# Attention inside a fused transformer layer: sums behind the second half's scores, maxima between the halves, the last two PSUM banks paired anew

## The reference

```python
xn = _layernorm(x)
q, k, v = split(einsum('bte,fe->btf', xn, in_proj))        # 16 heads of 8
a = softmax(q / sqrt(8) @ k.T + causal mask)
attn = (a @ v) @ out_proj.T
w = top-2 of softmax(xn @ wr.T + rb), normalised
ffn = expert_shared(xn) + sum_e w[:, e] * expert_e(xn)     # silu(h@g.T) * (h@u.T) @ d
out = x + attn + ffn
```

## Time and profile before

| | |
|---|---|
| time, median of 3 runs | 467.42 us (467.25 to 471.32) |
| profiled execution, span from first to last instruction | 485.8 us |
| front, to the first exponential | 44.3 us |
| attention, 64 steps | about 226 us |
| experts, from the last exponential | about 216 us |
| PE busy / DVE / ACT / POOL | 439.9 / 359.8 / 312.8 / 302.7 us |

### The profile page before, as it was taken

The page is one execution under the profiler, slowest core; times in us unless marked ns, Lnnn a source line. Parts: engine busy times, 40 slices in busy tenths (PEclk is TensorE's granted clock), DMA queues, the critical chain, the costliest instruction groups (busy, mean ns, idle before and its releaser), DMA issues.

```text
span 485.8 us, 12527 instructions
## 1 busy us (share of the span) xinstructions
PE 439.9 (91%) x3983; PEld 329.3 (68%) x3987; DVE 359.8 (74%) x804; ACT 312.8 (64%) x709; POOL 302.7 (62%) x439
## 2 busy tenths in 40 slices
PE   8888897988998989999889999998999899979995
PEld 4666565665666666666555688786877788868884
DVE  6885997987878877778774387585765777566987
ACT  2756676775867677767677676565565766555552
POOL 1326887997887888887888500755547487845300
PEclk9999999998999999999999999999999999989998
DMA  8776798999875555666356337787777767821762
GB/s 233 229 240 233 230 329 294 295 332 331 266 232 153 156 164 174 173 177 168 119 165 255 90 84 214 242 290 225 225 234 247 239 195 258 299 60 35 245 204 65
DMA packets 60415, 102.00 MB, mean 210 GB/s; under 512 B 11045, under 2 KB 29226, under 8 KB 59328
## 3 DMA queue, kind: packets, MB, share of 16 engines
q1 hardware_dynamic: 55872, 92.74, 61.2%
q0 software_dynamic: 4480, 8.47, 5.2%
HBM read 62.49 MB, written 39.46 MB: 210 GB/s over the span
## 4 chain that ended last, share of the span: by engine, by line
PE 62%; ACT 7%; POOL 6%; issue 5%; DVE 4%; SPq 4%; DMA 2%; another core or an unknown queue 2%; DVEq 0%; ACTq 0%; POOLq 0%
PE ps L850 11%; PE ps L848 11%; PE ps L849 11%; PE ps L917 6%; PE ps L978 6%; PE ps L925 4%; ACT sb_work L706 4%; POOL sb_work L620 3%; POOL xs L596 2%; PE ps L998 2%; DMA sb_ring<-qk 2%; PE ps L1143 2%; PE ps L981 2%; SPq L471 2%
## 5 line engine op out<-in xcount | busy, mean ns | idle before, releaser
L1343 DVE TENSOR_REDUCE sb_blockmax<-ps 128x6 f32<-128x768 f32 x128 | 121.5, 956 | 37.2 <-PE ps L925 32.4
L706 ACT ACTIVATE sb_work<-ps 128x768 f32<-128x768 f32 x128 | 104.7, 818 | 64.7 <-PE ps L913 63.5
L648 POOL DMA_INDIRECT ys<-sb_v_all,sb_xn_all x76 | 81.3, 1069 | 72.3 <-DVE sb_v_all L1464 52.6
L620 POOL TENSOR_SCALAR_AFFINE_SELECT sb_work<-sb_work 128x512 f32<-128x512 f32 x128 | 82.2, 646 | 27.6 <-ACT sb_work L706 25.5
L849 PE MATMUL ps<-sb_ring,sb_wb 128*128 128x512 f32 (+1 forms) x231 | 83.6, 362 | 0.0
L1443 DVE TENSOR_TENSOR sb_v_all<-ps,sb_v_all 128x512 f32<-128x512 f32 (+1 forms) x93 | 57.5, 618 | 24.4 <-ACT sb_v_all L796 10.6
L596 POOL DMA_INDIRECT xs<-sb_xn_all,sb_posu x64 | 62.9, 983 | 10.6 <-issue 10.6
L917 PE MATMUL ps<-sb_ring 32*128 32x256 f32 x256 | 49.5, 377 | 20.7 <-ACT sb_work L706 10.1
L796 ACT ACTIVATE sb_v_all<-ps 128x512 f32<-128x512 f32 (+1 forms) x93 | 49.7, 534 | 10.5 <-PE ps L850 5.4
L917 PEld LDWEIGHTS ps<-sb_ring 32*128 32x128 f32 x256 | 25.6, 183 | 44.9 <-issue 38.4
L848 PE MATMUL ps<-sb_ring,sb_wb 128*128 128x512 f32 (+1 forms) x138 | 51.6, 374 | 3.3 <-issue 1.8
(11 more groups left out here) (168 smaller groups left out, 1089.0 us busy)
## 6 DMA issues: line engine op xcount, KB each, us to landing
sb_wb<-wd SPq DMA_DIRECT2D x75, 384.0 KB
sb_ring<-qk SPq DMA_DIRECT2D x64, 256.0 KB
wd<-sb_wb SPq DMA_DIRECT2D x8, 1152.0 KB, 5.9
xs<-sb_o_all SPq DMA_DIRECT2D x19, 260.0 KB, 4.2
qk<-sb_ring SPq DMA_DIRECT2D x32, 128.0 KB
sb_work<-ys SPq DMA_DIRECT2D x16, 256.0 KB, 3.2
sb_xn_all<-xs SPq DMA_DIRECT2D x15, 260.0 KB
sb_o_all<-w SPq DMA_DIRECT2D x8, 384.0 KB, 3.9
```

Source lines behind the costliest of these rows:

```text
L620: pool.affine_select(out=o, in_=o, compare_op=ALU.is_ge, fill=0.0, base=0, pattern=[[0, 4], [1, 128]], channel_multiplier=-1)\
L648: pool.indirect_dma_start(out=ys_d, out_offset=bass.IndirectOffsetOnAxis(ap=row, axis=0), in_=yst[i % NYS][:, EMB * j:EMB * j + EMB], in_o ...
L706: act.activation(part.rearrange("p (k h q) -> p h k q", h=2, q=128), ps[:, 4:6, 0:HEAD].rearrange("p h (k q) -> p h k q", q=128), ACT.Exp, ...
L1343: dve.tensor_reduce(blockmax[:, a:b + 1, 0:3], ps[:, a:b + 1, 0:HEAD].rearrange("p h (k c) -> p h k c", c=128), AX.X, ALU.max).then_inc(s[ ...
```

## The change

The banks are paired anew: X becomes bank 6 and J bank 7. Sums go to X beside the transposes, and side products go to J beside the maxima (the last sums, of n = 63, go to J). On PE `sums(n - 1)` moves from before `scores(n, 1)` to behind it. `maxima` moves from the end of step n, where it served quad n + 2, to between the halves, where it serves quad n + 1. On ACT the copy of the queries moves between the two exponentials, the copy of the sums no longer waits for the maxima but comes behind the side copy, and the copy of the values moves from n mod 4 = 0 to n mod 4 = 2 of the sequence before. No instruction is added or removed; DVE, POOL and SP keep their order.

```diff
-        J, X = ps[:, 6, :], ps[:, 7, :]
+        X, J = ps[:, 6, :], ps[:, 7, :]
...
+        def summed_out(n):
+            return (X if n < NQ - 1 else J)[:, 256:512]
...
+            def summed(n):
+                act.wait_ge(s["PV"], n + 1)
+                if isq(n - 1):
+                    act.wait_ge(s["T"], n)
+                act.activation(ot[:, :], summed_out(n), ACT.Copy).then_inc(s["OT"], 1)
...
                     for k, pair in enumerate(PAIRS[::-1]):
-                        if k and isq(n - 2):
-                            unscaled(n - 2)
+                        if k:
+                            if isq(n - 2):
+                                unscaled(n - 2)
+                            queries(n + 1)
                         act.wait_ge(s["ST"], 2 * n + k + 1)
...
+                if isq(n - 1):
+                    summed(n - 1)
                 c = turned(n)
...
-                if isq(n - 1):
-                    act.wait_ge(s["PV"], n)
-                    if isq(n + 2):
-                        act.wait_ge(s["Mt"], n + 3)
-                    if isq(n - 2):
-                        act.wait_ge(s["T"], n - 1)
-                    act.activation(ot[:, :], J[:, 256:512], ACT.Copy).then_inc(s["OT"], 1)
-                if n >= 0:
-                    queries(n + 2)
...
             def step(n):
...
-                if n == 0:
-                    maxima(1)
                 if isq(n - 2):
-                    bank_read(n - 1)
                     pe.wait_ge(s["OT"], n - 1)
...
                     last.then_inc(s["T"], 1)
+                if isq(n) and isq(n + 1):
+                    maxima(n + 1)
+                if isq(n) or isq(n + 3):
+                    scores(n, 1)
                 if isq(n - 1):
                     sums(n - 1)
-                if isq(n) or isq(n + 3):
-                    scores(n, 1)
                 if n > -4:
                     bank_read(n - 1)
-                if isq(n - 2) and has_side(n):
-                    pe.wait_ge(s["xc"], n - 1)
-                side(n)
-                if n >= 0 and isq(n + 2):
-                    maxima(n + 2)
+                if has_side(n):
+                    if isq(n):
+                        pe.wait_ge(s["q4b"], min(n + 2, NQ))
...
+                    side(n)
```

More of the change, by code:

```diff
@@ L692, in unscaled, with own_values @@
                 act.activation(xo[c % 2][:, :, j, :, :], view[:, :, :, 0:HD + 1], ACT.Copy).then_inc(s["xc"], 1)
+            def summed(n):
[3 more added lines that the diff above has]
+                act.activation(ot[:, :], summed_out(n), ACT.Copy).then_inc(s["OT"], 1)
+            def own_values(b):
+                act.wait_ge(s["lg"], b + 1)
+                act.wait_ge(s["v1"], 2)
+                if b >= 2:
+                    act.wait_ge(s["PV"], 4 * (b - 1))
+                act.activation(v_sb[b % 2][:, :, :, 0:HD],
+                               v_all[:, 2 * b:2 * b + 2, :].rearrange("p s (h d) -> p s h d", h=HEADS), ACT.Copy)\
+                    .then_inc(s["va"], 1)
             def step(n):
@@ L708, in step @@
                                        scale=SCALE).then_inc(s["ex"], 1)
-                        if n == 0 and k == 0:
-                            queries(1)
                 if j in (0, 1) and isb(b + 3):
@@ L729, in step @@
                         .then_inc(s["cnt"], 1)
-                if isq(n - 1):
-                    act.wait_ge(s["PV"], n)
-                    if isq(n + 2):
-                        act.wait_ge(s["Mt"], n + 3)
-                    if isq(n - 2):
-                        act.wait_ge(s["T"], n - 1)
-                    act.activation(ot[:, :], J[:, 256:512], ACT.Copy).then_inc(s["OT"], 1)
-                if n >= 0:
-                    queries(n + 2)
-                if j == 0 and isb(b):
-                    act.wait_ge(s["lg"], b + 1)
-                    act.wait_ge(s["v1"], 2)
-                    if b >= 2:
-                        act.wait_ge(s["PV"], 4 * (b - 1))
-                    act.activation(v_sb[b % 2][:, :, :, 0:HD],
-                                   v_all[:, 2 * b:2 * b + 2, :].rearrange("p s (h d) -> p s h d", h=HEADS), ACT.Copy)\
-                        .then_inc(s["va"], 1)
+                if n == 0:
+                    own_values(0)
+                if n >= 0 and j == 2 and isb(b + 1):
+                    own_values(b + 1)
                 if n == 2:
@@ L970, in sums @@
                 b, j = quad(n)
-                if isq(n + 2):
-                    pe.wait_ge(s["q4b"], n + 3)
+                if isq(n - 1):
+                    pe.wait_ge(s["xc"], n)
+                    pe.wait_ge(s["OT"], n)
                 pe.wait_ge(s["sel"], 2 * n + 2)
@@ L976, in sums @@
                 p = P[n % 2].rearrange("p (a k h q) -> p a h k q", a=2, h=2, q=128)
+                out = summed_out(n)
                 for h in range(4):
-                    pe.matmul(J[32 * h:32 * h + 32, 256:512], v_sb[b % 2][:, 0, 4 * j + h, :],
+                    pe.matmul(out[32 * h:32 * h + 32, :], v_sb[b % 2][:, 0, 4 * j + h, :],
                               p[:, h // 2, h % 2, 1:3, :], start=True, stop=False, skip_group_check=True)
                 for h in range(4):
-                    last = pe.matmul(J[32 * h:32 * h + 32, 384:512], v_sb[b % 2][:, 1, 4 * j + h, :],
+                    last = pe.matmul(out[32 * h:32 * h + 32, 128:256], v_sb[b % 2][:, 1, 4 * j + h, :],
                                      p[:, h // 2, h % 2, 0, :], start=False, stop=True,
@@ L1023, in tokens_across, with idle @@
                 last.then_inc(s["xT"], 1)
-            def idle(count):
+            def idle(count, out=J):
                 for _ in range(count):
-                    pe.matmul(X[:, :], busy[:, 0:128], busy[:, :], start=True, stop=True, skip_group_check=True)
+                    pe.matmul(out[:, :], busy[:, 0:128], busy[:, :], start=True, stop=True, skip_group_check=True)
             pe.wait_ge(s["busy"], 1)
@@ L1054, in _ @@
             maxima(0)
-            idle(2)
+            idle(2, X)
             pe.wait_ge(s["lg"], NB)
```

9 lines of the change are left out of this document (5 added, 4 removed).

## The result

The changed kernel takes **472.23 us** in the median of 20 runs (470.4 to 474.9), the kernel before on the same chip 467.15 us (20 runs, 465.11 to 471.32). The ratio is 1.0104, with a 95% interval of 1.0083 to 1.0125: **slower by 1%**, 5.1 us, where 3.0 us less was forecast. The time lies above the range, 457 to 471.

A forecast was written before the change was run, and what follows sets the result against it. Attention steps were taken as bound by mask, sums and scores in series, and by ACT where a side product stands. Gains 2.1 + 0.8 + 0.9 + 0 - 0.2 - 0.6 = 3.0 us: 467.4 to 464.4 us, range 457 to 471.

The forecast's parts named there:

- part three: Steps with n mod 4 = 2 and 3 take 3.15 and 3.25 us; a four-step sequence 13.70 against 13.83 now.
- the zero for steps 0 to 23: No gain, as DVE's routing and transfers hold these steps; bounds a gain of 4 us and a loss of 2.
- So 6 x 0.13 = 0.8 us gained: Steps 28 to 51: six sequences fall from 13.83 to 13.70 us each.
- 0.9 in steps 24 to 27: This one sequence falls from 14.60 to 13.70 us, 0.9 gained.
- steps 52 to 60: Nine steps without side product, POOL their floor, at 3.20 us: 28.8 against 30.9, 2.1 us gained.
- Rival B: VectorE's late remainder delays maxima and second scores in 26 side steps, 0.4 us each: 10.4 us more, 474.8; chance 0.13.
- the side steps: Steps with a side product (n mod 4 = 0 or 1, to n = 49): second half 2.15 us, held by ACT.
- In steps 61 to 63 ... I take 0.2.: Sums stand in front of the first expert's matmuls: a 0.2 us loss, at most 0.79.
- Step 34's 0.6: Second exponential 2.61 us after the first, ACT idle for PE, cause unknown: about 0.6 us expected to be paid again.
- the first half: From a step's first exponential to its second: 1.50 us, no longer waiting for POOL's mask and the sums.
- Rival A: ACT does not hold side steps, whose second half ends with PE at 1.87 us: 7.3 us more gained, 457.1; chance 0.22.
- Rival C: The loop gets no shorter, the halves exchanging what they have: 467.4 us, give or take 1; chance 0.13.

The follow-up runs named there:

- experiment 5: Changed kernel with VectorE's routing piece moved from between the two maxima to the step's end: 494.13 us, 1.0218; with side product ahead of sums too, 488.19 us, 1.011.
- after: First profile of the changed kernel, no further edit: span 472.7 us; median of its timed runs 472.23 us.
- before_again: Kernel before, unchanged, profiled again on a chip of the 485 us sort: 485.2 us against 486.03, ratio 1.000.
- experiment 4: Changed kernel with VectorE's small reductions of the maxima ahead of the side product's remainder: 494.17 us, 1.012, and 493.0 us, 1.0143.
- before_two: Kernel before, unchanged, profiled on a chip of the 467 us sort: 467.52 us, ratio 1.0035, span 465.2 us.
- before: Profile of the kernel before that the forecast was made from, on a chip of the 485 us sort: span 485.8 us.
- side_first_three: Changed kernel with the side product ahead of the sums on PE, on a chip of the 485 us sort: 490.73 us, 1.0101.
- neg_first_two: Changed kernel with VectorE's small reductions of the maxima ahead of the side product's remainder, second run: 493.0 us against 483.61, 1.0143.
- route_last: Changed kernel with VectorE's routing piece moved to the step's end: 494.13 us against 482.63, 1.0218.
- best_again: Changed kernel with side product ahead of sums, ACT's turned copy ahead of the sums' copy, values' copy between the exponentials: 482.69 us, 0.9993.
- best_third: Changed kernel with side product ahead of sums, ACT's turned copy ahead of the sums' copy, values' copy between the exponentials: 487.87 us, 1.0048.
- ot_first: Changed kernel with ACT's sums' copy ahead of its side copy: 493.19 us against 486.03, 1.0114.

## Why the prediction was wrong

**The steps that failed are the subtraction in part three and the zero for steps 0 to 23.**

*"So 6 x 0.13 = 0.8 us gained", and 0.9 in steps 24 to 27.* The minuend came from one execution, 18.4 us above the median that was to be predicted, and I took it that its surplus lay elsewhere. Part of it lay here. On the chip of 467 us a sequence before takes 81.11 / 6 = 13.52, not 13.83, and steps 24 to 27 take 13.91, not 14.58. Against 13.83 measured for the changed kernel that is 6 x 0.31 = 1.9 us lost, and 0.1 gained. The minuend was mis-sized by 1.9 and 0.7, the changed kernel's own term by 0.8 (13.70 for 13.83). In steps 52 to 60 both were mis-sized alike, 30.9 for 30.20 and 28.8 for 27.70, and the difference came out nearly right by that. Even the trace that I had showed how thin this term was: 0.13 in 13.8.

*"I take 0" for steps 0 to 23, "nearest to the loaded engines", with a loss of 2 at the most.* Measured are 3.8. The bound of 2 priced twelve side products at 0.15 each and nothing else. The side steps' second halves lose more than that even in the quiet stretch: 2.20 for 1.91 with n mod 4 = 0 and 2.19 for 1.60 with n mod 4 = 1, which the forecast never compared. The other second halves lose 0.27 and 0.37. So the second halves of steps 0 to 23 lose 6.9 us. In steps 28 to 51 the first halves give 7.2 back; here they give 3.1. "DVE's routing and the transfers hold them, and the order on both is unchanged" was true and beside the point: what VectorE does is unchanged, but the changed kernel asks for its result earlier. Before, the maxima for the queries after next stood last in a step; now those of the next queries stand ahead of the second scores, so a delay of VectorE's small reductions lands on the exponentials. The first halves of steps 12, 15, 16 and 20 take 2.22 + 2.31 + 2.64 + 2.13 = 9.30 us, against 7.84 before and 5.8 without routing pieces in front (experiment 5). So 1.5 us of the loss is the change's, nearly all of it in steps 15 and 16 (1.71 and 1.67 before); in steps 12 and 20 the kernel before had long first halves too, 2.04 and 2.42.

The granted clock blurs the split of the 3.8. The changed kernel had 0.53 in step 16's second half (3.33 us, where `after` took 2.20); the kernel before had 0.77 in steps 0 and 1 (7.41 us, where `before_again` took 6.19 at 1.00). Three executions of before took 41.64 to 44.27 us in steps 0 to 11, two of the changed kernel 43.71 and 47.28. So each row of the table is known to about 1 us there.

Rival B named this mechanism, VectorE coming late for the maxima and the second scores, but I priced it only where the remainder delays it, in the side steps of a quiet stretch. There it does not occur, as forecast. In steps 12 and 15 it does (experiment 4).

*"In steps 61 to 63 ... I take 0.2."* Behind the last exponential 1.1 us are lost. The new wait in front of the sums makes step 63's sums wait for ACT's unscaled copy (L696), and ACT does the table load and an instruction of the experts first. The changed kernel:

```profile
266.85 0.81 ACT L729 ACTIVATE sb_work<-ps 128x768 f32<-128x768 f32 x1 [0.51 <-PE ps L923]
268.40 1.28 ACT L664 ACT_TABLE_LOAD   x1
270.29 0.22 ACT L696 ACTIVATE sb_xo<-ps 128x72 f32<-128x72 f32 x1
270.56 0.64 PE L991 MATMUL ps<-sb_work 128*32 128x256 f32 x8 [0.98 <-ACT sb_xo L696]
```

Before, they started 265.06 - 263.19 = 1.87 us after the last exponential, without a wait; now 3.71 us after it, and PE stands still for 0.98. The sums of step 62 (0.79) also lie behind that exponential now. How the 1.1 divides between the two is not shown. The wait guards bank X, which ACT reads there, but the last sums go to J, so by the banks alone they could do without it; no run leaves it out. I had moved the sums in my head but had not followed the new wait for `xc` past the loop's end.

*Step 34's 0.6 "again"*. On the chip of 467 us this first half of before takes 1.98 us, not 2.61, and the changed kernel has none above 1.70 in steps 24 to 60. The trace that I had shows where the 0.6 lies: PE's last group of scores starts at 169.70 and ends at 169.93, but the exponential starts only at 170.73, 1.03 us after that start. In `before_two` the distance is 0.28:

```profile
169.70 0.23 PE L913 MATMUL ps<-sb_ring 32*128 32x128 f32 x2
165.92 0.22 PE L913 MATMUL ps<-sb_ring 32*128 32x128 f32 x2
166.20 0.81 ACT L706 ACTIVATE sb_work<-ps 128x768 f32<-128x768 f32 x1 [0.95 <-PE ps L913]
```

This is not one step's accident. In steps 24 to 60 the distance in front of the second exponential never exceeds 0.28 in `before_two`, but is above 0.4 in 22 of the 37 steps of the profile that I forecast from, and in 23 of `before_again`; in steps 0 to 23 it is 0.27 in the median of all three. So much of the minuend's surplus was a delay of the slower chips between PE's record and ACT's start (see the last section).

*What was right:* the first half (1.50; 1.45), the side steps (2.15; 2.20), the other two (3.15 and 3.25; 3.18 and 3.31), steps 52 to 60 (2.1; 2.5), and that PE, once relieved, is not what holds the side steps. Rival A fell: its 1.87 needed the side product first, and with it the half is 1.85. Rival C fell by its reasons, since the first half did shorten to 1.45, though its picture of halves that exchange what they have is what the table shows. The measured time lies near B's 474.8, but by luck: B's wait is absent in the side steps that it priced.

The bounds 461.0 to 468.0 do not follow from the forecast's own terms either: a gain of 4 and a loss of 2 around 464.4 give 460.4 to 466.4 by themselves.

On the chips of 485 us the same order costs more (1.011 to 1.022 for its near relatives), see below.

## What to carry to other kernels

When a term is the difference of two nearly equal times, take both from executions of the same length as the time that is to be predicted, or let the range carry the whole surplus of the profile. When work is moved ahead on one engine, list what every other engine must now deliver earlier, and price that in each stretch of the program, the busiest first; that the producer's own order is unchanged says nothing. And put what another engine waits for ahead of what can run late: the side product before the sums gave 8.3 us where the kernel before takes 467. But what is put ahead must be ready itself: in step 6, where that product waits for VectorE, the same order cost 1.1 us.

## What the runs showed of the hardware

The two sorts of chip differ in waits, not in how long VectorE works. It is busy 359.8 us in both `before` and `before_two`. In the experts' part its most frequent addition takes 618 ns on the one and 617 on the other, but it waits 10.1 us longer, 4.4 of that for PE. What in the chips makes the difference is not shown. The line group of before from the last exponential on, span 485.8 us:

```profile
L1443 DVE TENSOR_TENSOR sb_v_all<-ps,sb_v_all 128x512 f32<-128x512 f32 (+1 forms) x93 | 57.5, 618 | 24.4 <-ACT sb_v_all L796 10.6 <-PE ps L850 7.5 <-remote 3.5
```

and of `before_two`, span 465.2 us:

```profile
L1443 DVE TENSOR_TENSOR sb_v_all<-ps,sb_v_all 128x512 f32<-128x512 f32 (+1 forms) x93 | 57.4, 617 | 14.3 <-ACT sb_v_all L796 9.9 <-PE ps L850 3.1
```

In the attention the wait between PE's record and ACT's start is longer there. In `side_first_three` (485 us sort), step 34, the sums' last group starts at 167.34, but ACT's copy of them starts 0.96 us later, where in step 54 of the changed kernel (467 us sort, the first two rows) it started 239.19 - 238.73 = 0.46 later:

```profile
238.73 0.40 PE L994 MATMUL ps<-sb_work 128*32 128x128 f32 x8
239.19 0.39 ACT L703 ACTIVATE sb_ot<-ps 128x256 f32<-128x256 f32 x1 [0.32 <-PE ps L994]
167.34 0.40 PE L994 MATMUL ps<-sb_work 128*32 128x128 f32 x8
168.30 0.38 ACT L703 ACTIVATE sb_ot<-ps 128x256 f32<-128x256 f32 x1 [0.82 <-PE ps L994]
```

Of the 18 second halves with n mod 4 = 2 or 3 in steps 24 to 59, 11 are over 2.0 us in this run, 11 in `neg_first_two` and `route_last`, 5 in `best_again` and `best_third`, none in `before` or `before_again`, and one in the five profiles taken on chips of 467 us. The kernel before is not spared: its sums stand in the first half, and there the delay shows, in front of the second exponential. On the chip of 467 us its first halves with n mod 4 = 1, 2 and 3 take 1.54, 1.71 and 1.72 us in steps 24 to 51, and 1.69, 1.86 and 1.86 in `before`. In these kernels the delays begin where POOL begins to send tokens. PE's record shows no gap at that place, so what delays it is not shown; that it has to do with the sends is only argued. With it goes that the side product's place gives 1.7% on the one sort of chip (0.9946 for 1.0119), and on the other 0.5% beside `ot_first` (1.0063 for 1.0114) and 1.1% beside `route_last` (1.011 for 1.0218); the changed kernel itself was not run there.
